# Order of three accumulating matmuls in a masked-softmax aggregation on one core: high·high, low·high, high·low becomes high·high, high·low, low·high

## What is computed

```
left   = (context @ W_common.T) @ w_left  + b_left        # one number per row
right  = (context @ W_common.T) @ w_right + b_right
logits = left[:, None] + right[None, :]
logits = where(logits >= 0, logits, 0.2 * logits)
logits = where(adj <= 0, -inf, logits)
coefs  = softmax(logits, axis=-1)                         # 8192 x 8192
h      = relu(coefs @ x)
out    = layernorm(x + h)                                 # over the 256 columns
```

## Time and profile before

| | |
|---|---|
| median of 3 runs | 1517.51 us (1517.49 to 1521.56) |
| the profiled execution, its own time | 1518.96 us |
| its span, first to last instruction | 1517.2 us |
| PE (matmul) busy | 1385.1 us, 91%, 12334 matmuls |
| PEld (weight loads) busy | 1207.3 us, 80%, 12334 loads |
| DVE (VectorE) busy | 1317.8 us, 87% |
| ACT (ScalarE) busy | 645.2 us, 43% |
| POOL (GpSimd) busy | 88.8 us, 6% |
| DMA | 329.59 MB, mean 217 GB/s |
| granted TensorE clock over the span | 0.958 of full |

### The profile page before, as it was taken

One profiled execution on the slowest core, in us unless ns is written; L12 is line 12 of the kernel. 1 busy time (PEld: TensorE's weight loads), 2 busy tenths in 40 slices (PEclk: granted clock), 3 DMA queues, 4 the chain that ended last, 5 costly groups with the idle time before them and its releaser, 6 DMA issues.

```text
span 1517.2 us, 28376 instructions
## 1 busy us (share of the span) xinstructions
PE 1385.1 (91%) x12334; PEld 1207.3 (80%) x12334; DVE 1317.8 (87%) x1178; ACT 645.2 (43%) x690; POOL 88.8 (6%) x214
## 2 busy tenths in 40 slices
PE   1007699999999999999999999999999999999998
PEld 0005588888888888888888888888888888888887
DVE  6759899988998999989998989899998989899881
ACT  0194444443444444443444444344444444444430
POOL 0033000000000000000000000000000000000000
PEclk7558899999999999999999999999999999999999
DMA  9972998989889898989888898989889888988860
GB/s 386 336 167 78 224 234 210 241 213 233 218 220 224 209 230 211 239 215 232 220 218 223 213 225 214 233 220 233 220 219 226 212 225 215 231 217 219 209 168 11
DMA packets 86544, 329.59 MB, mean 217 GB/s; under 512 B 19728, under 2 KB 44304, under 8 KB 52624
## 3 DMA queue, kind: packets, MB, share of 16 engines
q1 hardware_dynamic: 81776, 321.47, 82.8%
q10 hardware_dynamic: 4640, 6.29, 1.5%
HBM read 319.29 MB, written 8.39 MB: 216 GB/s over the span
## 4 chain that ended last, share of the span: by engine, by line
PE 89%; DVE 4%; SPq 3%; DMA 2%; ACT 1%; issue 0%; POOL 0%; POOLq 0%; DVEq 0%
PE ps L352 30%; PE ps L349 30%; PE ps L350 29%; SPq L213 3%; DVE X L615 2%; DMA T<-in_x_dram 2%; DVE strip L652 1%; DVE T L696 1%; DVE tab L518 1%; DMA strip<-in_adj_dram 0%; PE ps L316 0%; ACT strip L423 0%; DMA wcol<-in_L_gnn_w_left_dram 0%; ACT X L394 0%; ACT gw L389 0%
## 5 line engine op out<-in xcount | busy, mean ns | idle before, releaser
L349 PE MATMUL ps<-X,T 128*128 128x257 f16 x4096 | 1117.5, 273 | 38.5 <-DVE T L696 38.4
L350 PE MATMUL ps<-X,T 128*128 128x257 f16 x4096 | 1114.6, 273 | 0.0
L352 PE MATMUL ps<-X,T 128*128 128x257 f16 x4032 | 1107.6, 275 | 0.0
L423 ACT ACTIVATE strip<-strip 128x2048 f32<-128x2048 f32 x256 | 489.2, 1911 | 505.7 <-DMA strip<-in_adj_dram 505.4
L696 DVE STREAM_TRANSPOSE T<-strip 128x2048 f32<-128x2048 f32 x256 | 588.8, 2301 | 74.3 <-PE ps L352 74.3
L652 DVE SCALAR_TENSOR_TENSOR strip<-tab,arow,strip 128x2048 f32<-128x2048 f32 x256 | 597.9, 2336 | 51.5 <-ACT strip L423 50.8
L349 PEld LDWEIGHTS ps<-X,T 128*128 128x128 f16 x4096 | 405.6, 99 | 91.9 <-issue 21.1
L350 PEld LDWEIGHTS ps<-X,T 128*128 128x128 f16 x4096 | 399.9, 98 | 60.8
L352 PEld LDWEIGHTS ps<-X,T 128*128 128x128 f16 x4032 | 391.1, 97 | 54.7
L404 ACT ACTIVATE xs<-ps,small 128x256 f32<-128x256 f32 x64 | 30.3, 473 | 158.2 <-DVE small L701 158.2
L304 POOL TENSOR_SCALAR small<-small 128x1 f32<-128x1 f32 x64 | 12.2, 190 | 1311.6 <-ACT xs L412 1311.6
(11 more groups left out here) (96 smaller groups left out, 250.7 us busy)
## 6 DMA issues: line engine op xcount, KB each, us to landing
strip<-in_adj_dram SPq DMA_DIRECT2D x1016, 256.0 KB, 4.7
xs<-in_L_gnn_context_dram SPq DMA_DIRECT2D x15, 1024.0 KB, 9.7
T<-in_L_gnn_context_dram SPq DMA_DIRECT2D x4, 2048.0 KB, 16.7
X<-in_L_gnn_context_dram SPq DMA_DIRECT2D x4, 2048.0 KB, 34.1
xs<-in_x_dram SPq DMA_DIRECT2D x64, 128.0 KB, 5.1
out_dram<-xs SPq DMA_DIRECT2D x64, 128.0 KB, 5.1
xs<-in_x_dram SPq DMA_DIRECT2D x4, 512.0 KB, 27.8
xs<-in_x_dram ACTq DMA_DIRECT2D x4, 512.0 KB, 20.0
```

The source lines that it names most:

```text
L349: nc.tensor.matmul(ps[o][:, 0:D + 1], hi, X16[:, jb, 0:D + 1], start=(i == 0), stop=False)
L350: nc.tensor.matmul(ps[o][:, 0:D + 1], lo, X16[:, jb, 0:D + 1], start=False, stop=False)
L352: m = nc.tensor.matmul(ps[o][:, 0:D + 1], hi, X16[:, jb, D + 2:2 * D + 3], start=False, stop=(i == JB - 1))
L423: nc.scalar.activation(s, s, ACT.Relu, scale=KEEP).then_inc(s_m, 1)
```

## The change

In each block of groups 1 to 63 the product of high weights and low x moves from the third place to the second, and the product of low weights and high x from the second to the third. The three products, their operands and their accumulator are the same ones. The mark that ends the accumulation (`stop`) is now on the low-weights product of the last block, and this is the one that raises `s_mm`. In group 0 the mark stays on the last matmul at L360.

```diff
                     nc.tensor.matmul(ps[o][:, 0:D + 1], hi, X16[:, jb, 0:D + 1], start=(i == 0), stop=False)
-                    nc.tensor.matmul(ps[o][:, 0:D + 1], lo, X16[:, jb, 0:D + 1], start=False, stop=False)
                     if g > 0:
-                        m = nc.tensor.matmul(ps[o][:, 0:D + 1], hi, X16[:, jb, D + 2:2 * D + 3], start=False,
-                                             stop=(i == JB - 1))
+                        nc.tensor.matmul(ps[o][:, 0:D + 1], hi, X16[:, jb, D + 2:2 * D + 3], start=False, stop=False)
+                    m = nc.tensor.matmul(ps[o][:, 0:D + 1], lo, X16[:, jb, 0:D + 1], start=False,
+                                         stop=(g > 0 and i == JB - 1))
```

## The result

The changed kernel takes 1515.73 us against 1519.41 us of the kernel before (medians of 19 runs each, taken side by side). The ratio is 0.9973 with a 95% interval of 0.9966 to 0.998, so it is faster by 0.2 to 0.3%, some 4 us. One of the 19 executions of the changed kernel took 2161.39 us, at a granted clock of 0.647 where the others had 0.955 to 0.959, and the ratio leaves it out. The forecast was 1517.5 and no change, range 1502 to 1528. The time lies in the range; the effect lies just inside the 0.3% that was called no change, and its interval does not contain 1. That the number came within 1.8 us is in part luck: it stood on a median of 3 runs of the kernel before, 1517.51 us, and 19 runs of it give 1519.41.

The account below looks back on a forecast made before the run. TensorE's pace of starting matmuls was taken as the bound. Three gaps were to sum to an unchanged 333.3 ns a block over 4032 blocks, so the median stayed 1517.5 us; range 1502 to 1528, no change 0.47.

Parts of the forecast that it names:

- The bound: Middle of the kernel: TensorE's pace of starting matmuls sets the time, 333.3 ns a block; VectorE has room to 303.
- the terms put at nothing: Group 0, other engines' work, waits before a group and the tail after the last group: each unchanged, 0.
- The bounds: A block's three gaps in the new order sum to 328.9 to 335.9 ns: -17.7 to +10.5 us.
- A to C: Gap from high weights on high x to high weights on low x: between 109.1 and 113.5 ns.
- C to B: Gap from high weights on low x to low weights on high x: between 110.9 and 113.5 ns.
- B to A: Gap from low weights on high x to the next block's high on high: 108.9 ns, from group 0.
- the forecast's second reason: Per block, x and weights change halves equally often in both orders, counted round the ring: 333.3 ns stays.
- the ring argument: The new order is the old cycle of three products run backwards, with equal changes of half: block unchanged at 333.3 ns.
- Its first reason: A gap is no fixed price of its pair; group 0's 0.10 and 0.12 us turns suggest delay saved and paid elsewhere.
- Rival 1: Faster, gaps belong to pairs: 331.5 ns a block, 1510 us, or 1504 at group 0's pace; chance of faster 0.35.
- Rival 2: High weights followed by a change of x half cost 113.5 ns: 335.9 a block, 1528 us; nearly all of slower's 0.18.
- Rival 3: Loading the same weights again costs or saves by itself; if it could not overlap, 391 us more, 1 in 100.

Follow-up runs that it names:

- bc256: Changed order, x halves aligned to 16 bytes, low-on-high and high-on-low products 256 columns wide instead of 257: 1499.76 us, ratio 0.9874 to the kernel before.
- a8_before: Order of the kernel before, with rows of x 1040 bytes and the low half at byte 520: 1514.91 us, ratio 0.997.
- a8_after: Changed kernel's order, with rows of x 1040 bytes and the low half at byte 520: 1515.94 us, ratio 0.997 to the kernel before.
- a16: Rows of x 1056 bytes, both halves at multiples of 16 bytes: 1507.18 us in the changed order, 1506.68 us in the order of before.
- off8: Changed order, rows of 1056 bytes, every product starting 8 bytes past a multiple of 16: 1505.08 us, ratio 0.9909 to the kernel before.
- x_after_w_before: Changed kernel with weights loaded in the order of before (high, low, high), x in the changed order, old addresses: 1514.83 us, ratio 0.9971.
- x_before_w_after: Kernel before with high and low weights exchanged between second and third product, x order kept, old addresses: 1519.99 us, ratio 1.0003.

## Why the prediction was right, and where it was not

**The bound** was right: with 3605 instead of 3594 blocks in the same 1200 us, the time follows the starts of TensorE, and the terms put at nothing stayed so where the rows show them. From the last matmul to the store are 1513.19 - 1508.97 = 4.22 us, as in 1514.96 - 1510.74 = 4.22 before. In the experiments up to 5.0 ns less a block (bc256, 328.6) came through to the end, at about 1499.8 us, so VectorE did not take over.

**The bounds** of the sum, 328.9 to 335.9 ns, held; the load lines give 332.5. A to C, taken between 109.1 and 113.5, is 109.7. C to B, between 110.9 and 113.5, is 113.4. B to A, read from group 0 as 108.9, is 109.4.

**The step that failed is the forecast's second reason**, that a block costs by how often x and the weights change halves, counted round the ring, whichever way the ring runs. It left the block at 333.3 ns where it became 1.0 shorter, and so missed 4.0 us, which is why the number is right only within its bound of 0.3%. The run with x of the changed order and weights of before shows what counts in its place: the sequence of x's start addresses modulo 16, in which the two orders differ (0 0 4 8 8 12 and 0 4 0 8 12 8). The last paragraph of the prediction had named this outcome, a block that changes though both halves are visited as often; its explanation, the direction of a step, does not fit as it stands, since each order takes one step of x from high to low in a block and one back, and the weights have no part. What differs is the addresses: after C the start goes from 4 to 8 or from 12 to 0 before, and from 4 to 0 or from 12 to 8 in the changed order. Where both orders have the same sequence round the ring (a8_before and a8_after), or no difference at all (a16), the ring argument gives the right answer.

**Its first reason**, that delay is saved up and paid elsewhere, was half right. The gaps are indeed no fixed price of a pair: a step from 8 to 8 is 110.0 where all starts are alike (off8) and 112.4 from A to B in the odd blocks of before, and in two passes dear and cheap gaps make up for each other. But the row it leaned on was misread: the 0.10 and 0.12 by turns are 109.8 and 112.5 ns, and the turns are even and odd blocks, so they show the address and not by themselves a delay that is carried along. And the total is not firm.

**Rival 1** named the right direction and, with the nearest row for each gap, 331.5 ns and 1510 us. Its gain is too large by 1.0 ns, of which 0.6 are A to C (109.1 taken, 109.7 found) and 0.5 B to A, with 0.1 back at C to B. **Rival 2** decided itself at A to C: 109.7, not above 112. **Rival 3** is settled at nothing: A to C is 109.7 with the same weights (the changed kernel) and with others (x_after_w_before), and equal weights on equal x cost and save nothing either (x_before_w_after).

**What stays open** is why a single product of three with another start costs some 2 ns a block (332.3 against 330.2), before's sequence 3.4 and the changed one 2.3, while pairs 0 0 8 8 cost 0.2 for two products. The runs fix the prices, not the mechanism inside the engine. The length of a row was changed together with the place of the low half, and no run has rows of 1056 bytes with unequal starts or rows of 1040 with equal ones. Against the length as the cause speaks that the dear gap of a8_after lies between two products on one and the same row, C and B.

## What to carry to other kernels

Where TensorE starts a product every 110 ns, try to let all streamed operands of a chain start at the same place modulo 16 bytes: lengthening the row of x from 1032 to 1056 bytes made this kernel 0.9% faster (1507 us), three times what the reordering gave, and then the order no longer matters. Before reasoning about an order, work out the distance between starts line by line from the loads' lengths and idle times: equal products at unequal distances say that something other than the arithmetic is being paid. And look at a single column over a round number: the 257th cost 0.9 ns here, twice its share of 1/2.4 = 0.42. Finally, sort equal products by what differs in their addresses before averaging them, since a mean of 110.9 was here one of 109.4 and 112.4.

## What the runs showed of the hardware that was not expected

- The distance between two matmuls depends on the start addresses of the streamed operand: 110.0 ns each when all start alike modulo 16 bytes (at 0 or at 8). With rows of 1040 bytes and one product of three starting elsewhere it is 113.6 to 114.0 behind that product and 109.1 to 109.5 at the two others, and 4 and 8 bytes off cost the same (a block 332.3 ns). With rows of 1032 bytes 109.0 to 113.8 were found.
- The weights, their halves and their repetition have no influence on it that could be measured (3605 and 3594 blocks follow x's order in both crossed kernels).
- With equal starts a product takes 109.1 ns at 256 columns, 110.0 at 257 and 112.4 at 264. Against one column in 1/2.4 ns that is 2.4 ns more at 256 and at 264, and 2.9 at 257.
- After TensorE's 17 us wait the granted clock of the stretch 163 to 170 us was 0.76 in one profile and 0.50 in another, and the group that started there took 22.9 and 24.1 us, 1.2 us of difference.
